# One gather of source rows for both attention passes in a four-layer graph kernel

## The reference

```python
xp = (x @ W).reshape(n, 3, 128)
a_src = einsum('nhc,hc->nh', xp, att_src)
a_dst = einsum('nhc,hc->nh', xp, att_dst)
alpha = leaky(a_src[row2] + a_dst[col2] + a_edge)     # per edge, and one loop per node
attn = segment_softmax(alpha, col2)                   # over the edges that end in a node
agg = segment_sum(attn[:, :, None] * xp[row2], col2)
y = agg.reshape(n, 384) @ lin_W + lin_b
h = x + y
return layernorm(h) * ln_g + ln_b
```

## Time and profile before

| | us |
|---|---|
| median of 3 runs (9837.43 to 9849.79) | 9839.8 |
| profiled execution | 9843.85 |
| its span, first to last instruction | 9842.1 |
| busy in the span: DVE | 7417.1 |
| POOL | 7419.2 |
| PE | 6205.4 |
| ACT | 5851.3 |
| mean granted clock of PE, as a share of full speed | 0.717 |

### The profile page before, as it was taken

How to read it: one execution, slowest core, us unless ns; L and a number is a source line. 1 busy time by engine, 2 the same in 40 slices (tenths; PEclk the granted TensorE clock), 3 DMA queues, 4 the chain that set the end, 5 groups by cost and what they waited for, 6 DMA issues and landing times. The chain is left out here.

```text
span 9842.1 us, 131500 instructions
## 1 busy us (share of the span) xinstructions
PE 6205.4 (63%) x32436; PEld 5091.6 (52%) x32436; DVE 7417.1 (75%) x22799; ACT 5851.3 (59%) x13869; POOL 7419.2 (75%) x6901
## 2 busy tenths in 40 slices
PE   7017766668874666787736666884467676654444
PEld 3016655656664666677736666783234453432222
DVE  8349989979997877799978888565568776864444
ACT  0016667779998999899948887331135443432222
POOL 7756678876658888688847776776777777777777
PEclk9559988889995555688868888655568656765555
DMA  3999988863336777444425554563346443432222
GB/s 100 332 298 314 315 284 311 311 209 104 101 91 216 241 243 240 163 159 159 154 91 185 185 185 164 167 176 96 95 133 192 131 119 107 145 106 67 68 67 61
DMA packets 1024295, 1693.85 MB, mean 172 GB/s; under 512 B 301775, under 2 KB 544661, under 8 KB 1023474
## 3 DMA queue, kind: packets, MB, share of 16 engines
q1 hardware_dynamic: 797008, 1380.40, 41.2%
q0 software_dynamic: 166560, 199.56, 9.5%
q10 hardware_dynamic: 59970, 105.49, 3.1%
HBM read 988.10 MB, written 707.84 MB: 172 GB/s over the span
## 5 line engine op out<-in xcount | busy, mean ns | idle before, releaser
L1357 POOL DMA_INDIRECT g_got<-scaled,row_src x2352 | 2227.2, 947 | 789.1 <-issue 664.5
L909 DVE SCALAR_TENSOR_TENSOR g_sums<-g_got,first,g_sums 128x128 f32<-128x128 f32 (+3 forms) x3136 | 874.3, 279 | 1117.3 <-DMA g_got<-scaled,row_src 1106.7
L301 PE MATMUL g_a_p_z<-sb_L_gnn_W,g_a_u_t 128*128 128x128 f32 (+3 forms) x2574 | 586.4, 364 | 564.7 <-ACT g_a_u_t L1190 175.3
L913 DVE SCALAR_TENSOR_TENSOR g_sums<-g_sums,cont,g_got 128x128 f32<-128x128 f32 (+3 forms) x3128 | 881.5, 282 | 0.0
L1190 ACT COPY g_a_u_t<-g_a_p_t 128x512 f32<-128x512 f32 (+3 forms) x495 | 225.1, 455 | 1103.3 <-PE g_a_p_t L1142 643.6
L301 PE MATMUL g_bb_p_z<-sb_L_gnn_W,g_bb_u_t 128*128 128x128 f32 (+2 forms) x4302 | 750.4, 334 | 121.1 <-DVE g_bb_z L1084 66.0
L301 PEld LDWEIGHTS g_a_p_z<-sb_L_gnn_W,g_a_u_t 128*128 128x128 f32 (+1 forms) x2574 | 430.3, 238 | 732.0 <-ACT g_a_u_t L1190 413.4
L301 PEld LDWEIGHTS g_bb_p_z<-sb_L_gnn_W,g_bb_u_t 128*128 128x128 f32 x4302 | 661.6, 233 | 178.8 <-issue 150.1
L1190 ACT COPY g_bb_u_t<-g_bb_p_t 128x1024 f32<-128x1024 f32 (+2 forms) x294 | 234.0, 796 | 842.9 <-PE g_bb_p_t L292 842.0
L2497 POOL DMA_INDIRECT gb_got<-x,row_src x392 | 410.7, 1048 | 228.0 <-POOLq L179 124.0
L461 POOL DMA_INDIRECT f_got<-in_x,idx_dst x396 | 460.2, 1162 | 139.5 <-issue 120.1
(11 more groups left out here) (494 smaller groups left out, 23115.8 us busy)
## 6 DMA issues: line engine op xcount, KB each, us to landing
raw<-gb_u SPq DMA_DIRECT2D x98, 768.0 KB, 3.9
xs<-f_o ACTq DMA_DIRECT2D x97, 516.0 KB
f_x<-in_x ACTq DMA_DIRECT2D x97, 512.0 KB
g_bb_own<-in_x SPq DMA_DIRECT2D x97, 512.0 KB
wide<-g_bb_o SPq DMA_DIRECT2D x97, 512.0 KB
g_bb_own<-wide SPq DMA_DIRECT2D x97, 512.0 KB
g_bb_res<-in_x SPq DMA_DIRECT2D x97, 512.0 KB
x<-g_bb_o SPq DMA_DIRECT2D x97, 512.0 KB
```

The costliest lines, as they stand in the source:

```text
L301: last = nc.tensor.matmul(dst_psum[0:p, q * g * width:(q * g + n) * width], turned_tile[0:n * k, q * P:q * P + p], weight[0:n * k, 0:n * w ...
L909: nc.vector.scalar_tensor_tensor(out=self.firsts, in0=new, scalar=first[:, col], in1=self.firsts, op0=ALU.mult, op1=ALU.add).then_inc(run_ ...
L913: nc.vector.scalar_tensor_tensor(out=self.part(b.s, c), in0=before, scalar=cont[:, col], in1=new, op0=ALU.mult, op1=ALU.add).then_inc(run_ ...
L1357: pool.indirect_dma_start(got[b.s4][:, c * row:(c + 1) * row], None, table, bass.IndirectOffsetOnAxis(ap=index[:, b.n * CH + c:b.n * CH + ...
```

## The change

The table `att` and the scores of b rows in the node pass are gone: no turn, evacuation, multiplication, copy and store for them. The score pass gathers whole rows of x2 by source into four buffers `got`. PE turns the four columns of a block, ACT evacuates them, PE multiplies them by the three source columns of `score_w`, and DVE copies the 12 columns of scores into `att_e`, now laid out by head. SP stores each gathered block in a new table `x2_e`, ordered by edge. The edge pass has no gathers: SP loads blocks of `x2_e` (256 KB, 2 KB per partition). There POOL adds the bias to x (`add_base`), and DVE adds that to the product in one instruction instead of two. The order and the lags of POOL's and SP's stages in the edge pass change with it: `weigh_own` from lag 1 to 0, `add_beta` from 4 to 2, `store_sums` from 1 to 3 and behind the loads.

```diff
-        att = dram("att", [NA + N, 4])
+        x2_e = dram("x2_e", [P, T * D])
...
-        att_e = keep("att_e", [P, T * 4])
+        att_e = keep("att_e", [P, 3, T])
...
                     dve.wait_ge(m.scored, b.n + 1)
-                    dve.wait_ge(self.other.scored, min(b.n + 1, NB))
-                    if b.after(2):
-                        dve.wait_ge(m.stored_b[b.s], b.pair * DMA)
-                    both = self.p_sc[0:p, 0:j * 6].rearrange("p (j f) -> p j f", f=6)
-                    if self.a:
-                        nc.vector.tensor_copy(own_src[:, :, bass.ds(b.n * CH, CH)], both.rearrange("p j f -> p f j")[:, 0:3, :])
-                        nc.vector.tensor_copy(own_dst[:, :, bass.ds(b.n * CH, CH)], both.rearrange("p j f -> p f j")[:, 3:6, :])
-                    nc.vector.tensor_copy(split(self.att_s[b.s], p, j, 4)[:, :, 0:3], both[:, :, 0:3]).then_inc(m.attended, 1)
+                    both = self.p_sc[0:p, 0:j * 6].rearrange("p (j f) -> p f j", f=6)
+                    nc.vector.tensor_copy(own_src[:, :, bass.ds(b.n * CH, CH)], both[:, 0:3, :])
+                    nc.vector.tensor_copy(own_dst[:, :, bass.ds(b.n * CH, CH)], both[:, 3:6, :]).then_inc(m.attended, 1)
...
                     if b.after(2):
                         act.wait_ge(m.stored[b.s], b.pair * DMA)
-                        act.wait_ge(m.turned, b.n - 1)
+                        if self.a:
+                            act.wait_ge(m.turned, b.n - 1)
                     self.n2.scale(self.o_s[b.s], self.y_s[b.n % 4], b, self.first, p, j).then_inc(m.normed_b, 1)
...
                     def _(sp):
                         pipeline(sp, [(na.load, 0, NBA), (nb.load, 0, NB), (na.load_again, 4, NBA), (nb.load_again, 4, NB),
-                                      (na.store, 7, NBA), (nb.store, 7, NB), (na.store_scores, 9, NBA),
-                                      (nb.store_scores, 9, NB)])
+                                      (na.store, 7, NBA), (nb.store, 7, NB)])
                         na.stores_done()
                         nb.stores_done()
...
-                        pipeline(dve, [(na.scores, 9, NBA), (nb.scores, 9, NB), (stats_1, 2, NBA), (factors_2, 6, NBA),
+                        pipeline(dve, [(na.scores, 9, NBA), (stats_1, 2, NBA), (factors_2, 6, NBA),
                                        (na.shift, 5, NBA), (nb.shift, 5, NB), (na.rectify, 5, NBA), (nb.rectify, 5, NB),
...
                         pipeline(act, [(n2.root, 6, NBA), (na.normalise_1, 3, NBA), (nb.normalise_1, 3, NB), (n1.root, 2, NBA),
-                                       (na.normalise_2, 6, NBA), (nb.normalise_2, 6, NB), (na.evacuate, 7, NBA),
-                                       (nb.evacuate, 7, NB)])
+                                       (na.normalise_2, 6, NBA), (nb.normalise_2, 6, NB), (na.evacuate, 7, NBA)])
...
-                        pipeline(pe, [(na.turn, 7, NBA), (nb.turn, 7, NB), (na.score, 8, NBA), (nb.score, 8, NB)])
+                        pipeline(pe, [(na.turn, 7, NBA), (na.score, 8, NBA)])
...
+                n, r, m, e = AttentionNode(sb, ps, rows_b), rows_b, mark_b, mark_a
+                got = [sb(f"got{s}", [P, CH * D]) for s in range(UNROLL)]
+                got_t = sb("got_t", [D, SLOTS])
+                p_e = ps("p_e", [P, SLOTS])
...
                         def gather(b):
+                            if b.after(UNROLL):
+                                pool.wait_ge(e.turned, b.n - UNROLL + 1)
+                                pool.wait_ge(raw_stored[b.s4], b.turn * DMA)
                             for c in range(CH):
                                 pool.indirect_dma_start(
-                                    att_e[:, 4 * (b.n * CH + c):4 * (b.n * CH + c + 1)], None, att,
+                                    got[b.s4][:, c * D:(c + 1) * D], None, x2,
                                     bass.IndirectOffsetOnAxis(ap=row_src[:, b.n * CH + c:b.n * CH + c + 1], axis=0)
                                 ).then_inc(gathered[b.s4], DMA)
 
                         pipeline(pool, [(n.add_beta, 2, NB), (gather, 0, NBE)])
-                        for s in range(UNROLL):
-                            pool.wait_ge(gathered[s], past(gathered[s]) + blocks_in(NBE, s, UNROLL) * CH * DMA)
...
-                        pipeline(sp, [(load, 0, NB), (n.store, 6, NB), (n.store_next, 8, NB)])
+                        def store_edges(b):
+                            sp.wait_ge(gathered[b.s4], gathers_before(gathered[b.s4], b))
+                            sp.dma_start(x2_e[:, b.n * CH * D:(b.n + 1) * CH * D], got[b.s4][:, :]
+                                         ).then_inc(raw_stored[b.s4], DMA)
+
+                        pipeline(sp, [(load, 0, NB), (store_edges, 2, NBE), (n.store, 6, NB), (n.store_next, 8, NB)])
                         n.stores_done()
+                        for s in range(UNROLL):
+                            sp.wait_ge(raw_stored[s], blocks_in(NBE, s, UNROLL) * DMA)
...
-                        pipeline(dve, [(rows, 3, NB), (n.stats_1, 3, NB), (n.factors_2, 6, NB), (n.gain, 5, NB), (n.add_x, 5, NB),
+                        def take_scores(b):
+                            dve.wait_ge(e.scored, b.n + 1)
+                            nc.vector.tensor_copy(att_e[:, :, bass.ds(b.n * CH, CH)],
+                                                  p_e[:, 0:CH * 3].rearrange("p (c f) -> p f c", f=3)).then_inc(e.attended, 1)
+
+                        pipeline(dve, [(rows, 3, NB), (take_scores, 2, NBE), (n.stats_1, 3, NB), (n.factors_2, 6, NB), (n.gain, 5, NB), (n.add_x, 5, NB),
                                        (n.stats_2, 5, NB), (n.factors_1, 3, NB), (n.out_rows, 8, NB)])
...
-                        pipeline(pe, [(n.next_weight, 8, NB), (n.turn_out, 7, NB), (multiply, 2, NB), (turn, 1, NB)])
+                        def turn_edges(b):
+                            pe.wait_ge(gathered[b.s4], gathers_before(gathered[b.s4], b))
+                            if b.after(1):
+                                pe.wait_ge(e.attended, b.n)
+                            turn_chunks(p_e, got[b.s4], D).then_inc(e.turned, 1)
+
+                        def score_edges(b):
+                            pe.wait_ge(e.evacuated, b.n + 1)
+                            for c in range(CH):
+                                last = nc.tensor.matmul(p_e[:, c * 3:(c + 1) * 3], got_t[:, c * P:(c + 1) * P], score_w[:, 0:3],
+                                                        start=True, stop=True)
+                            last.then_inc(e.scored, 1)
+
+                        pipeline(pe, [(score_edges, 2, NBE), (n.next_weight, 8, NB), (n.turn_out, 7, NB), (multiply, 2, NB),
+                                      (turn, 1, NB), (turn_edges, 1, NBE)])
...
-                        pipeline(act, [(evacuate, 2, NB), (n.root_2, 6, NB), (n.normalise_1, 4, NB), (n.root_1, 3, NB),
+                        def evacuate_edges(b):
+                            act.wait_ge(e.turned, b.n + 1)
+                            if b.after(1):
+                                act.wait_ge(e.scored, b.n)
+                            nc.scalar.copy(got_t[:, :], p_e[:, :]).then_inc(e.evacuated, 1)
+
+                        pipeline(act, [(evacuate, 2, NB), (evacuate_edges, 2, NBE), (n.root_2, 6, NB), (n.normalise_1, 4, NB), (n.root_1, 3, NB),
                                        (n.evacuate_out, 7, NB), (n.normalise_2, 6, NB)])
...
-                att_h = att_e[:, :].rearrange("p (t f) -> p f t", f=4)[:, 0:H, :]
+                att_h = att_e[:, :, :]
...
-                        def gather(b):
-                            if b.after(UNROLL):
-                                pool.wait_ge(weighed, b.n - UNROLL + 1)
-                            for c in range(CH):
-                                pool.indirect_dma_start(
-                                    got[b.s4][:, c * D:(c + 1) * D], None, x2,
-                                    bass.IndirectOffsetOnAxis(ap=row_src[:, b.n * CH + c:b.n * CH + c + 1], axis=0)
-                                ).then_inc(gathered[b.s4], DMA)
+                        def add_base(b):
+                            pool.wait_ge(m.gained, b.n + 1)
+                            x = split(n.x_r[b.s], P, CH)
+                            nc.gpsimd.tensor_tensor(x, x, row_of(gat_row, P, CH), ALU.add).then_inc(rows_based, 1)
...
-                        pipeline(pool, [(gather, 0, NBE), (weigh_own, 1, NBA), (gather_firsts, 1, NBA), (n.add_beta, 4, NBA)])
+                        pipeline(pool, [(weigh_own, 0, NBA), (gather_firsts, 1, NBA), (n.add_beta, 2, NBA),
+                                        (add_base, 2, NBA)])
...
+                        def load_edges(b):
+                            if b.after(UNROLL):
+                                sp.wait_ge(weighed, b.n - UNROLL + 1)
+                            sp.dma_start(got[b.s4][:, :], x2_e[:, b.n * CH * D:(b.n + 1) * CH * D]
```

(29 more changed lines are left out.)

24 lines of the change are left out of this document (9 added, 15 removed).

## The result

The changed kernel takes **9997.6 us** (median; 9990.1 to 10006.2), the kernel before 9843.7 in the same series: ratio 1.0154, 95% interval 1.0142 to 1.0167. It is 154 us slower; 9969 was forecast, in a range of 9700 to 10070. The profiled execution has a span of 9994.1 us (9842.1 before).

The account below looks back on a forecast made before the run. ACT was taken to bound the node and score passes, a loop of DVE's sums, SP's store and the load the edge pass. From 9843.85 us, -88 + 85 - 1 + 133, less 4, gave 9969 us, range 9700 to 10070.

Parts of the forecast that it names:

- the step that costed it: Node pass: ACT loses the evacuation of b, 0.90 us of pitch in each of 98 ticks, 88 us less.
- a ring of PE and ACT as said: Score pass: scores wait for ACT's new copy, ACT's next copy for PE's turn of the edges, closing once per tick.
- the clock's share: Score pass: low-clock ticks make ACT wait 2.0 us; counted as 39 us of the 85 us more.
- the PE tick plus ACT's copy and the handovers, about 1.0 us, 7.8 us. At full clock it fits in 8.84.: Score pass: PE's 6.8 us plus 1.0 us makes a 7.8 us loop, hidden under ACT's 8.84 us tick.
- I take one tick in five: Score pass: share of ticks taken to have PE's low clock, 0.4 us x 98 = 39 us.
- my comparison of 2 us with 2.83: Score pass: PE idles about 2 us per tick, less than the 2.83 us after which its clock fell.
- Rival 2: Score pass: PE's clock falls in every tick; +157 us on the forecast, 10126 us; chance 0.06.
- Edge pass, what goes: Edge pass: the 0.90 us load wait and one 0.68 us addition leave DVE's tick, 10.61 to 9.03 us.
- Edge pass, what comes: Edge pass: own_w, released by gb_u, and x_beta stall DVE's nmr by 2.94 us; tick 11.97 us, 133 us more.
- such a DVE instruction stands until POOL's run of SBUF work ends, four instructions here: Edge pass: DVE's nmr, reading two SBUF operands, is held through POOL's whole own_w, 2.5 us of stall.
- the four signs: Signs of the summed terms: node pass -88, score pass +85, softmax -1, edge pass +133 us.
- Rival 1: Edge pass: own_w not released by gb_u, stalls near zero, ACT's 9.1 us tick; -148 us, total 9688 us; chance 0.24.

Follow-up runs that it names:

- experiment 6: Changed kernel plus four, six or eight extra 128x128 matmuls per PE tick in the score pass; the profiled execution with four took 10000.4 us.
- experiment 1: Changed kernel with own_w one tick later in the edge pass (weigh_own lag 1 instead of 0): 9809.3 us, ratio 0.9955 to the kernel before.
- Experiment 3: Kernel before, with SP's load of x_r put ahead of the store of the sums in the edge pass: 9777.4 us, ratio 0.9929.

## Why the prediction was right in sum, and where it was not

**Node pass: right.** -90 for -88, by the step that costed it (0.90 us of ACT's pitch), with POOL's remaining slack of 0.31 us as worked out (10.12 - 9.81).

**Score pass: a ring of PE and ACT as said, but another one, and the clock's share too small.** The step that failed first is "the PE tick plus ACT's copy and the handovers, about 1.0 us, 7.8 us. At full clock it fits in 8.84." The ring that closes does not run through PE's whole tick and back over turn_edges; it leaves PE at turn_out, passes through ACT's copy of p_o, and then through 4.89 us of ACT's own queue (4505.49 to 4510.38). At the upper clock the other half, from the copy of gathered rows to that of p_o, takes 4.44 us (4506.66 to 4511.10 in the run of experiment 6 with four free matmuls), so even then the tick is 4.44 + 4.89 = 9.33 us, not 8.84. The changed kernel has such ticks itself:

```profile
4542.83 0.58 ACT L2302 COPY ga_got_t<-ga_p_e 128x512 f32<-128x512 f32 x1
...
4544.38 1.98 PE L302 MATMUL ga_b_p_g<-sb_L_gnn_W,ga_b_o_t 128*128 128x64 f32 x16
4546.20 1.04 PE L293 MATMUL ga_b_p_o<-ident,ga_b_o 128*128 128x128 f32 x8
...
4552.16 0.58 ACT L2302 COPY ga_got_t<-ga_p_e 128x512 f32<-128x512 f32 x1
```

Between 4100 and 4900, 17 of its 75 ticks take 9.33 or 9.34 us, and no group of matmuls in them took longer than at the upper level. The other 58 all have such a group and take 9.80 to 12.04 us.

So the step "I take one tick in five" failed too: it is 58 of 75. The kernel before showed more than one in five already: 36 of 86 groups p_g between 4100 and 4900 took longer than 1.97 us, and ACT waited only 1.1 us for PE in all between 4150 and 4850. Nor did the pause tell the level, as my comparison of 2 us with 2.83 supposed. In the kernel before, a pause of 2.83 us stood ahead of both:

```profile
4476.37 1.97 PE L301 MATMUL ga_b_p_g<-sb_L_gnn_W,ga_b_o_t 128*128 128x64 f32 x16 [2.83 <-DVE ga_b_g L2143]
...
4493.08 3.64 PE L301 MATMUL ga_b_p_g<-sb_L_gnn_W,ga_b_o_t 128*128 128x64 f32 x16 [2.83 <-DVE ga_b_g L2143]
```

The 2.18 us by which the tick grew (8.37 to 10.55) are then 0.47 for ACT's copy, 0.49 for the ring at the upper clock (9.33 - 8.84), and 1.22 for the clock (10.55 - 9.33). The first is confirmed by the run whose tick is 8.85. The runs bound the others: cutting the ring gives back 1.38, raising the clock to 0.93 gives back 0.74. Rival 2 (the clock falls in every tick, +157 on the forecast) was nearer for this pass, 242 us against 208 measured, and was given 6 in 100.

**Softmax:** +2 for -1, within where I cut.

**Edge pass, what goes: right.** The wait for x_r ended, and 9.03 us for DVE's tick without stalls is nearly borne out by experiment 1: 9.25 with the second nmr's 0.36 us left in it, so 8.89. Experiment 3 shows that 71 us of this lay in SP's order and had nothing to do with gathering once.

**Edge pass, what comes: place right, size wrong.** own_w is released by gb_u and meets DVE's small instructions; undoing that one lag gives 199 us back. The step that failed is "such a DVE instruction stands until POOL's run of SBUF work ends, four instructions here". I took it from the beginning of the pass. In the steady tick nmr waits for one POOL instruction (0.76 us, of which 0.16 is its own), and then the two engines take turns. The trace agrees with the rule in the Trainium skill (SBUF - State Buffer, Who interferes with whom), by which a DVE instruction with two SBUF inputs and a GpSimd one that reads SBUF exclude each other for a whole instruction. I had weighed that rule and said the sum would be the same "within 0.1 us", since POOL's 3.04 us would be paid in three portions. It is not: the portion that falls on gain is paid by POOL, which has slack. Measured were 11.32 us for the tick shown and 11.11 in the mean, against 11.97. Only 0.65 of the 1.00 us between forecast and result is this step; the rest is that I took a tick of 10.61 us for the pass before, whose mean is 10.75, and that the first ticks of the changed pass are shorter than the one shown. Why four instructions went through in a row at the beginning of the pass stays open; no run was made for it.

**The sum.** Three of the four signs and the place of both losses were right; the sizes of the two losses were off by +123 and -98 us. Rival 1 (no collision) was named at the right price, -148 us for the edge pass: experiment 1 makes it true there, and (9.25 - 10.75) x 98 is -147. Its total of 9688 was not met, since the score pass stays as it is.

## What to carry to other kernels

When a step is added to a software-pipelined loop, follow the ring through the queues at the place where it is put: a step that waits for another engine, ahead of work that engine waits for, ties the two together once per tick. Here PE's lower clock then reached ACT in 58 of 75 ticks. Try the order and the lag before the idea is judged: here one lag and two places in a queue turned +154 us into -163. And give GpSimd's large SBUF work a release that puts it beside DVE's sums in PSUM; the same three multiplications cost DVE nothing there, and some 2 us a tick beside nmr, gain and add_x, which read SBUF twice.

## What the runs showed that I had not expected

- **The length of PE's pause does not tell the clock.** With a pause of 1.61 us in every tick and eight 128x128 matmuls right behind it the granted clock stayed at 1.00; with pauses of 0.48 and 0.51 us (six and eight matmuls ahead of the pause, the three-column score matmuls right behind it) it fell in many ticks, to 0.84 and 0.93 in the mean. In the changed kernel it fell between 4502 and 4503 (1.00 in the microsecond before, 0.50 in the one after), some 2 us after PE had taken up work again at 4500.39, not in the pause. What does tell it is not shown: between these runs the place of the extra matmuls and what they wait for changed together.
- **Extra PE work can make a kernel faster.** Four useless matmuls a tick took the cut score pass from 9.18 to 8.85 us a tick and the kernel from 9691.7 to 9651.8 us.
- **In the steady tick DVE and POOL hand over at single instructions**, and either can be the one that waits: own_w grew from 3.04 to 4.00 us while gain passed at 0.68 us.
